# Chunked slot attention on one core: both score products in one stretch of TensorE, inversions and gates in another order, constants made inside the first router

## The reference, cut to what matters

```python
x = x + 0.5 * ffn(layernorm(x), ...)      # router (top 8 of 64 experts), then the experts
x = x + attn(layernorm(x), Wq, Wk, Wv, Wg, Ws, Wo, g_norm_weight)
# attn: H = 16 heads, DK = M = 64, DV = 128, T = 256
z = cumlogsumexp(s, time);  p = exp(s - z);  g = exp(z[t-1] - z[t])
# per time step:  hk = hk * g + k (x) p ;  ok = q . hk        (slots of keys)
# pv = softmax(ok);  hv = hv * g + p (x) v ;  ov = pv . hv    (slots of values)
o = ov * rsqrt(mean(ov * ov) + eps) * g_norm_weight
o = o * (gate * sigmoid(gate));  out = o @ Wo
```

## Time and profile before

| | |
|---|---|
| median of 3 runs | 2640.36 us |
| the profiled execution | 2640.57 us |
| its span, first to last instruction | 2638.4 us |
| PE busy | 89% of the span |
| DVE busy | 66% |
| POOL busy | 47% |
| ACT busy | 34% |
| mean granted TensorE clock | 0.954 of full speed |
| first router | about 7 to 84 us |
| first experts | about 84 to 320 us |
| attention | about 320 to 1786 us |
| second router and experts, closing | about 1790 us to the end |

### The profile page before, as it was taken

One profiled execution on the slowest core, in us unless ns is written; L12 is line 12 of the kernel. 1 busy time (PEld: TensorE's weight loads), 2 busy tenths in 40 slices (PEclk: granted clock), 3 DMA queues, 4 the chain that ended last, 5 costly groups with the idle time before them and its releaser, 6 DMA issues. The chain is left out here.

```text
span 2638.4 us, 46098 instructions
## 1 busy us (share of the span) xinstructions
PE 2341.7 (89%) x18006; PEld 2076.9 (79%) x18006; DVE 1736.6 (66%) x3420; ACT 886.0 (34%) x1768; POOL 1241.8 (47%) x1214
## 2 busy tenths in 40 slices
PE   7656499999999999999999999987566489999998
PEld 7545388889899888989998889877554377888887
DVE  6433267888787788777887887766422266776654
ACT  5322133333333333333333333324322133333332
POOL 3477634555455555545554555452488521221111
PEclk9788799999999999999999999988799799999999
DMA  8989500000000000000000000004799500000000
GB/s 275 274 224 216 115 13 21 5 17 22 9 17 17 21 6 19 19 21 5 17 21 21 6 17 21 13 3 153 207 218 215 120 24 17 25 25 25 17 9 16
DMA packets 188230, 165.43 MB, mean 63 GB/s; under 512 B 28432, under 2 KB 180976, under 8 KB 187504
## 3 DMA queue, kind: packets, MB, share of 16 engines
q1 hardware_dynamic: 161072, 120.53, 14.9%
q0 software_dynamic: 24576, 37.77, 7.8%
q10 hardware_dynamic: 2368, 4.19, 0.5%
HBM read 115.84 MB, written 51.04 MB: 63 GB/s over the span
## 5 line engine op out<-in xcount | busy, mean ns | idle before, releaser
L947 POOL TENSOR_TENSOR a_orstd<-a_ms,minus_half 128x8 f32<-128x8 f32 x64 | 106.7, 1667 | 467.6 <-DVE a_ms L1120 467.6
L927 POOL TENSOR_SCALAR a_pick<-a_index,lut_row 128x258 f32<-128x258 int32 x240 | 280.8, 1170 | 24.3
L1113 DVE RECIPROCAL a_rz<-a_rz 128x256 f32<-128x256 f32 x128 | 215.6, 1716 | 0.0
L630 PE MATMUL e_psX<-ident,e_xg 128*128 128x128 f32 x256 | 61.7, 327 | 167.3 <-DMA e_xg<-rows,slot_tok 166.7
L746 DVE TENSOR_TENSOR e_hT<-e_psH,e_sil 128x128 f32<-128x128 f32 x128 | 37.2, 291 | 256.5 <-ACT e_sil L704 151.7
L630 PEld LDWEIGHTS e_psX<-ident,e_xg 128*128 128x128 f32 x256 | 30.7, 156 | 211.9 <-DMA e_xg<-rows,slot_tok 208.6
L930 POOL TENSOR_TENSOR a_found<-a_found,a_pick 128x258 f32<-128x258 f32 x240 | 177.4, 739 | 20.0
L600 POOL DMA_INDIRECT e_xg<-rows,slot_tok x128 | 129.9, 1015 | 93.5 <-POOLq L235 55.1
L958 ACT ACTIVATE a_v<-a_psA 128x512 f32<-128x512 f32 x128 | 76.5, 598 | 224.1 <-PE a_psA L1462 224.1
L1460 PE MATMUL a_psC<-wo_high,a_oT 128*128 128x256 f32 x512 | 150.2, 293 | 1.5 <-DVE a_oT L1066 1.5
L1460 PE MATMUL f_pair<-f_lnT,wguT 128*128 128x512 f32 (+1 forms) x352 | 143.7, 408 | 7.5 <-DVE f_lnT L1726 7.2
(11 more groups left out here) (279 smaller groups left out, 7857.3 us busy)
## 6 DMA issues: line engine op xcount, KB each, us to landing
e_wg<-in_L_ffn_w_gate SPq DMA_DIRECT2D x128, 128.0 KB
e_wu<-in_L_ffn_w_up SPq DMA_DIRECT2D x128, 128.0 KB
e_wd<-in_L_ffn_w_down SPq DMA_DIRECT2D x128, 128.0 KB
rows<-r_row SPq DMA_DIRECT2D x32, 320.0 KB, 2.8
stream_b<-r_zeros SPq DMA_DIRECT2D x11, 384.0 KB, 4.9
stream_c<-rows SPq DMA_DIRECT2D x33, 128.0 KB, 3.2
r_xt<-in_L_attn_hidden_states SPq DMA_DIRECT2D x16, 256.0 KB, 5.6
stream_a<-r_xt SPq DMA_DIRECT2D x16, 256.0 KB, 3.6
```

What stands on the lines that cost most here:

```text
L630: nc.tensor.transpose(psX[u][:, c, :], xg[:, e % U, c * P:(c + 1) * P], cst["ident"][:, :]).then_inc(turned[u], 1)
L927: nc.gpsimd.tensor_scalar(pick[:, :, :], index[:, :, :], float(c), w["lut"][:, c:c + 1], ALU.is_equal, ALU.mult).then_inc(picked, 1)
L947: nc.gpsimd.tensor_tensor(out=flat(orstd[:, :, :]), in0=ms[:, :], in1=cst["minus_half"][:, 0:TT * HQ], op=ALU.pow).then_inc(orstd_ok, 1)
L1113: nc.vector.reciprocal(rz[:, a, :], rz[:, a, :]).then_inc(rz_ok, 1)
```

## The change

- The constants are no longer made in a block of their own. `constants` returns a function that the first router's POOL list calls first; PE, DVE and ACT of both routers begin with a wait until the nine last results are counted (`made`, MADE = 9). The two small loads of `attention_weights` are issued by the first router's SP list, behind the 16 loads of x.
- `scores_a(n+1)` is cut into `own_scores` (8 matmuls on the diagonal blocks, into the banks of q and k) and `scores_below` (4 matmuls on the lower left block, into psD, no mask: ACT copies it, `below_copy`, L958's helper, two of 128x256). Both move up behind `scores_b(n)`, so that `scores_b`, `own_scores`, `scores_below` and `state_read` follow one another.
- `masked_first` becomes two of 128x512 for four of 128x384 and stands behind `masked_second`, ahead of the running sums and inversions.
- `output(n-1)` moves ahead of `over_j(n)`. `slots_read(n+1)` and `state_of_slots(n+1)` move from the next step's beginning to behind `over_j(n)`, ahead of `gate(n+1,0)`. The gates come last in the step; the next step begins with `value(n+2,0)` and `slots(n+2)`.
- `gate` waits for the masks, since it shares their banks. `over_j(n)` waits for `below_copy(n+1)`. `ov_ps` is raised once instead of twice.
- DVE: `add_output(n-1)` stands between the two `invert`. `low_of_stream` follows the two `gate`, and ACT's `high_of_stream` follows the two tanh. `squares(n)` stays last, now directly behind them. `turn_stream` uses psB[1] instead of psC[0].
- `bt` lies in the memory of `sq` instead of `at`; `state` in that of `below`.

```diff
@@ moe_router @@
+                for dst, src, here in late:
+                        sp.dma_start(dst, src).then_inc(here, 16)
...
+                act.wait_ge(cst["made"], MADE)
...
                 past.clear(pool)
+                if make:
+                    make(pool)
...
+                dve.wait_ge(cst["made"], MADE)
                 for j in range(S):
                     moments_of(j)
...
+                pe.wait_ge(cst["made"], MADE)
                 pe.wait_ge(gw_here, 16)
@@ attention, ACT @@
+                def below_copy(m):
+                    act.wait_ge(below_ps, m + 1)
+                    for p in range(2):
+                        copy(flat(below[:, p, :, :]), psD[:, p, 0:NH * P], below_ok)
...
                         key(n + 1)
+                        below_copy(n + 1)
                         turned_exps(n + 1)
-                        if (n + 1) % QPB == QPB - 1 and n + 2 < N:
-                            high_of_stream((n + 1) // QPB + 1)
...
                         gate_tanh(n + 1, 0)
                         gate_tanh(n + 1, 1)
+                        if (n + 1) % QPB == QPB - 1 and n + 2 < N:
+                            high_of_stream((n + 1) // QPB + 1)
@@ attention, DVE @@
                 def masked_first(m):
-                    for h in range(HQ):
-                        dve.wait_ge(at_ps, HQ * m + h + 1)
-                        nc.vector.tensor_tensor(out=at[:, h, :], in0=first_banks[h][:, 0:3 * P],
...
+                    masked(at, [psA[1 - m % 2], psA[m % 2]], m, at_ps, at_ok)
...
                     masked_second(n)
                     if ahead:
+                        masked_first(n + 1)
                         dve.wait_ge(pzt_ok, n + 1)
                         running_sum(n + 1, 0)
                         running_sum(n + 1, 1)
                         invert(n + 1, 0)
-                        if (n + 1) % QPB == QPB - 1 and n + 2 < N:
-                            low_of_stream((n + 1) // QPB + 1)
+                    if n > 0:
+                        add_output(n - 1)
+                    if ahead:
                         invert(n + 1, 1)
...
                     if ahead:
                         gate(n + 1, 0)
                         gate(n + 1, 1)
-                    if n > 0:
-                        add_output(n - 1)
-                    if ahead:
-                        masked_first(n + 1)
+                        if (n + 1) % QPB == QPB - 1 and n + 2 < N:
+                            low_of_stream((n + 1) // QPB + 1)
                     squares(n)
@@ attention, PE @@
                 def gate(m, t):
-                    if t == 0:
-                        pe.wait_ge(q_ok, m + 1)
-                    else:
-                        pe.wait_ge(k_ok, m + 1)
+                    pe.wait_ge(at_ok, 2 * m + t + 1)
...
                     if ahead:
                         value(n + 1, 0)
-                    slots_read(n)
-                    state_of_slots(n)
-                    if ahead:
                         slots(n + 1)
                     turn_back(n)
...
                     scores_b(n)
-                    state_read(n)
                     if ahead:
+                        scores_a(n + 1)
+                        scores_below(n + 1)
+                    state_read(n, ahead)
+                    if n > 0:
+                        output(n - 1)
+                    over_j(n)
+                    if ahead:
+                        slots_read(n + 1)
+                        state_of_slots(n + 1)
                         gate(n + 1, 0)
                         if (n + 1) % QPB == QPB - 1 and n + 2 < N:
                             turn_stream((n + 1) // QPB + 1)
                         gate(n + 1, 1)
-                    over_j(n)
-                    if n > 0:
-                        pe.wait_ge(lnTl_ok, ...)
-                        output(n - 1)
-                    if ahead:
-                        scores_a(n + 1)
```

More of the change, by code:

```diff
@@ L147, in moe_router @@
+    c["made"] = s_cut
+    return c, make
+def moe_router(nc, cst, tag, past, x_src, gate_w, rows, fresh, slot_tok, behind=(), make=None, late=()):
     NZ = 11
@@ L1253, in turn_exps, with own_scores @@
                     mm.then_inc(et_ps, 1)
+                def own_scores(lhs, rhs, banks, ready):
+                    for a in range(NH):
+                        for t in range(TT):
+                            for p in range(2):
+                                r, own = p * DK, slice(t * P, (t + 1) * P)
+                                mm = nc.tensor.matmul(banks[p][:, (a * TT + t) * P:(a * TT + t + 1) * P], lhs[r:r + DK, a, own], rhs[r:r + DK, a, own],
+                                                      start=True, stop=True)
+                                if a == NH - 1 and t == TT - 1:
+                                    mm.then_inc(ready, 1)
                 def scores_a(m):
@@ L1287, in scores_b, with state_read @@
                     pe.wait_ge(st_ok, n + 1)
-                    for a in range(NH):
-                        for t in range(TT):
-                            for p in range(2):
-                                r, own = p * M, slice(t * P, (t + 1) * P)
-                                mm = nc.tensor.matmul(psB[p][:, (a * TT + t) * P:(a * TT + t + 1) * P], emT[r:r + M, a, own], pzT[r:r + M, a, own],
-                                                      start=True, stop=True)
-                                if a == NH - 1 and t == TT - 1:
-                                    mm.then_inc(bt_ps, 1)
-                def state_read(n):
+                    pe.wait_ge(lnTl_ok, n // QPB + 1)
+                    own_scores(emT, pzT, psB, bt_ps)
+                def state_read(n, more):
                     if n > 0:
@@ L1371, in _ @@
                 turn_exps(0)
+                scores_a(0)
+                scores_below(0)
+                slots_read(0)
+                state_of_slots(0)
                 gate(0, 0)
                 gate(0, 1)
-                scores_a(0)
                 for n in range(N):
@@ L2024, in macaron @@
             past = moe_router(nc, cst, "r1_", Mem(nc, ctx), x, gate_w, rows, (stream_a, stream_b), slot_tok,
-                              [(as_source(piece), piece["src"], piece["here"]) for piece in early])
+                              [(as_source(piece), piece["src"], piece["here"]) for piece in early], make, late)
             high = {name: wmem.sb(f"w{name}_high", [P, cols], F32R) for name, cols in sizes}
```

163 lines of the change are left out of this document (79 added, 84 removed).

## The result

The changed kernel takes 2687.8 us (median of 4 runs, 2686.5 to 2689.2) against 2641.2 us (2638.1 to 2642.5) for the kernel before beside it: 1.0181 times as long, 95% interval 1.0169 to 1.0193. It is slower, as forecast, by 46.6 us where I had 36.9.

What follows compares the result with a forecast made beforehand. Attention was taken as bound by PE's own work. Ordinary steps +17.5, new sequences +20.7, first and last step +0.9, beginning +3.1, end +1, constants -6.3: +36.9 on 2640.57 gives 2677.5 us, range 2655 to 2695.

Steps and rivals of the forecast that it cites:

- The sign and the mechanism: Attention loop: joined scores save 0.47 us a step, but the chain behind the last gates makes PE wait 0.85; net slower.
- The ordinary step: From scores_b to scores_b: 22.61 us against 22.23, +0.38 each, +17.5 us over 46 steps.
- The seams: Between PE's pieces in smaller tiles: joining the scores saves 0.47 us a step; behind over_j 0 to 0.2 uncertain.
- the row that the prediction took for it: Value's first matmul at 0.34 us against 0.24 for the gates', read as the cost of changing tile form.
- The step ahead of a new sequence: In 15 steps value waits 2.2 us for the stream's low half: 24.39 us against 23.01, +1.38 each, +20.7.
- The clock: Rival: PE's idle times drop its clock, every step's gates run at 1.2 GHz, +180 us, 2857 us; chance 0.03.
- The beginning of attention: Before the loop, masks now follow the inversions: turn_back at 351.6 us, not 348.49, +3.1; PE idles some 4 us.
- The start: Before the first router, removing the blocks for constants and small loads brings -6.3 us, ends -5.2 and -6.5.
- The end: End of attention: output(62) stands ahead of over_j(63) in a chain of latencies; 0 to +3.0 us, taken +1.
- first and last step: Loop's two edge steps: last has the chain without value and slots, +1.6; first has no output, -0.7; together +0.9 us.
- The sum: Whole kernel: all terms together +36.9 us on 2640.57, giving 2677.5 us, 1.4% slower.
- Add_output's cover: In the loop, add_output ends at 7.15 us and PE comes to slots_read at 7.62: 0.47 us cover, costed at nothing.

Runs made afterwards that it cites:

- The experiment on the squares: Changed kernel with the sum of squares and its small follower moved ahead of the two gates on DVE: 2672.0 us, ratio 1.0129 to the kernel before.
- the one on the gates' place: Changed kernel with both gate projections moved ahead of the slots' read and the state on PE: 2612.3 us, ratio 0.9908 to the kernel before.
- the low half's experiment: Changed kernel with the next stream's high half copied between the two tanh and its low half made between the two gates: 2673.0 us, ratio 1.0132.
- the changed kernel with the squares doubled: Changed kernel with the sum of squares computed twice on DVE, first into a buffer nobody reads: 2745.8 us, ratio 1.0409 to the kernel before.
- the masks' experiment: Changed kernel with the first scores masked before the inversions ahead of the loop, not after: 2683.1 us, ratio 1.0167 to the kernel before.
- the added reduction: Sum of squares computed twice: changed kernel 2745.8 us; kernel before 2647.2; changed kernel with gates before slots' read, low half between gates, masks first 2614.2.
- two other kernels: Changed kernel with the squares moved ahead of the gates (8 of 15), 2672.0 us, and with the sum of squares computed twice (5 of 15), 2745.8 us.

## Why the prediction was right, point by point

**The sign and the mechanism** held. The joined scores save PE's seams, and the chain tanh, gate, squares, okn behind gates that now stand last eats more than that. The experiment on the squares shows the chain, the one on the gates' place shows both halves at once.

**The ordinary step**: 22.66 against 22.61 us. Its terms were further off than its sum, and that they cancel is luck. The work without waits was 21.76 by my sum and is 21.95 by the trace: over_j with its seam 1.88, not 1.80 (0.18 of seam, near the upper end of the 0 to 0.2 I gave), value 1.48, not 1.40, slots 1.44, not 1.41. The waits were 0.85 by my sum and are 0.71, of which 0.33 at the value projection, where I had 0.1, and 0.38 at the transposes. From the last gate matmul to the transposes it takes 3.80 us, where I had 3.89.

**The seams.** All 64-row pieces run without one between them, as read from scores_b, and scores_below's pairs do run side by side (0.45). The Trainium skill, "TensorEngine Tiling (Array Packing)", section Key Properties, says that changing the tiling mode drains TensorE, without a price. The trace agrees and prices it: 0.18 us behind over_j, 0.10 behind the gates, before the same 128x64 tiles. But the row that the prediction took for it, 0.34 against 0.24 us at the first matmul of value, doesn't show it. In the same step of the kernel before, the second value projection follows the transposes back, with full tiles on both sides:

```profile
1019.90 0.47 PE L1460 MATMUL a_psA<-wv_high,a_lnT 128*128 128x512 f32 x1
1020.21 0.39 PE L1461 MATMUL a_psA<-wv_low,a_lnT 128*128 128x512 f32 x1
```

Its first matmul takes 0.31 us, and the first gate matmul behind over_j takes 0.32 (995.77 to 996.09 above). So most of that 0.10 is paid at the beginning of a projection behind products or transposes of 128 columns, whether the tile's form changes or not. Joining the scores removed one such beginning; what it removed in switches of the form is seen at their exits.

**The step ahead of a new sequence**: 24.65 against 24.39 us in 11 of 15. The low half lets PE go on at 15.18 us from scores_b, not 15.05, and value with slots takes 2.95, not 2.81.

**The clock** was my rival of 0.03, with every step at half rate and 2857 us. It came in small: 4 falls of 3.4 us, 6 us in all. The step that failed: I asked the question only of idle times under a microsecond, and did not put the 2.2 us wait that I had forecast myself, 15 times, under it. By the Trainium skill, "TensorE: Matmul & The Clock Gate", second failure mode, short idle times between groups of matmuls can make the clock oscillate if they come often. The steps between the first and the last do not show it. There the clock fell around single waits of 2.07 us only. It did not fall around the 1.47 us of the low half's experiment, nor with the wait of 1.29 us that the changed kernel with the squares doubled has in its ordinary steps.

**The beginning of attention**: +4.86 against +3.1. The wait of some 4 us was right (3.89). That the clock would then be at half for the work behind it was not in the sum; the masks' experiment puts 2.6 us on it. Without it the term would have come out near +2.3, so the rest of it was 0.8 too high.

**The start**: -5.13 at the first gather, where I had -6.3 for the whole; the profiles of the kernels with the new start have 78.5 to 80.0, 5.1 to 6.6 less than 85.08. The whole difference of -8.27 up to attention contains 3.14 that I attribute to nothing, for the reason given above. **The end** was +1 in the sum and is -0.16; the first and last step +0.9 and +1.1.

**The sum** missed 10.6 us of 47.5: loop +12 (the new sequences +9.4, of which clock 6; ordinary steps +2.4; first and last +0.2), beginning +1.8, start -2.0, end -1.2. **Add_output's cover**, costed at nothing with 0.47 us of margin, held: in the step shown DVE ends it at 984.93 us, 0.69 ahead of L1331, and PE never waits there for it.

## What to carry to other kernels

Moving work to the end of a step moves its readers' start too. For every piece that a reordering puts last, add up the small operations between it and the next thing that the bound engine needs, and compare that with the work left to cover it, before counting what the reordering saves. Here, swapping two blocks on TensorE turned a loss of 47 us into a gain of 24 us (ratio 0.9908) with the same instructions. And the slack in front of a reader, taken from start to start, accounts for what the added reduction cost in three kernels; taken from the end of okn, it came out 0.1 us too small in the kernel before.

## What the runs showed of the hardware that I had not expected

- TensorE's granted clock fell from 2.4 to 1.2 GHz for 3.4 us at a single idle time of 2.07 us inside dense work, in 4 of 15 cases (8 and 5 of 15 in two other kernels), and in none of 15 at 1.47 us. Each fall cost 1.5 us. In the changed kernel the falls are evenly spaced, every fourth case.
- The price of changing the tile's form depends on what stands ahead of it: 0.18 us behind 128-column products in full tiles, 0.10 us behind 512-column ones. In the kernel before, the first over_j has the first scores right behind it, in 64x128 tiles, and takes 1.88 us too, against 1.70 in front of full tiles.
- The first matmul of a projection of 512 columns takes 0.31 to 0.32 us behind transposes or products in full tiles, where the next ones take 0.23: this cost comes without a change of the tile's form.
- Behind a wait, the four transposes back took 0.41 us until the next matmul, without one 0.36: the wait costs 0.05 us more than its length.
- The first experts' stretch varied between 231 and 238 us from execution to execution, which is as much as the whole effect of the new start (7.4 us, 5 to 10).
